# First attention of a four-layer chain: five of eight key tiles summed, all on GpSimd, and the denominators made behind the next unit's first key tile

## What is computed

```python
tokens = x.reshape(B, C, N).transpose(0, 2, 1)          # B=8, C=256, N=1024
qkv = (tokens @ w_proj + b_proj).reshape(B, N, 8, 96)   # 8 heads of 32
attn = softmax(einsum('bihd,bjhd->bijh', q, k) * 32 ** -0.5, axis=2)
res = einsum('bijh,bjhd->bihd', attn, v).reshape(B, N, 256)
out = res @ w_out + b_out + tokens
```

## Time and profile before

| | us |
|---|---|
| median of 3 executions | 3152.33 |
| the profiled execution, its own time | 3150.14 |
| its span, first to last instruction | 3148.4 |
| mean granted TensorE clock, share of full | 0.929 |
| TensorE matmul busy | 2668.8 (85%) |
| VectorE busy | 2200.9 (70%) |
| ScalarE busy | 1287.3 (41%) |
| GpSimd busy | 656.9 (21%) |

### The profile page before, as it was taken

The page is one execution under the profiler, slowest core; times in us unless marked ns, Lnnn a source line. Parts: engine busy times, 40 slices in busy tenths (PEclk is TensorE's granted clock), DMA queues, the critical chain, the costliest instruction groups (busy, mean ns, idle before and its releaser), DMA issues.

```text
span 3148.4 us, 43492 instructions
## 1 busy us (share of the span) xinstructions
PE 2668.8 (85%) x14974; PEld 1865.5 (59%) x14974; DVE 2200.9 (70%) x2403; ACT 1287.3 (41%) x1860; POOL 656.9 (21%) x405
## 2 busy tenths in 40 slices
PE   6889979899788897888879888888888898888993
PEld 4447754577545775467654676447764477644772
DVE  4776668666686676867678566785668766777666
ACT  2553325433354333543335333453334533255333
POOL 0520116102160022500225002340024300252011
PEclk8999989999899998999989999899989999999997
DMA  6100050000400004000040001300022000310016
GB/s 151 27 24 1 0 128 1 24 1 14 115 1 24 1 14 115 1 24 1 23 106 1 24 1 42 87 1 24 1 64 65 24 1 1 92 38 24 1 54 240
DMA packets 46389, 124.58 MB, mean 40 GB/s; under 512 B 9792, under 2 KB 21312, under 8 KB 42560
## 3 DMA queue, kind: packets, MB, share of 16 engines
q1 hardware_dynamic: 46144, 121.41, 14.1%
HBM read 43.01 MB, written 23.86 MB: 21 GB/s over the span
## 4 chain that ended last, share of the span: by engine, by line
PE 59%; issue 13%; DVE 11%; ACT 4%; SPq 4%; POOL 4%; DMA 3%; DVEq 0%; ACTq 0%; POOLq 0%
PE tile L1352 23%; PE pv L1352 10%; POOL acc L619 4%; PE tile L1611 4%; PE tile L1430 4%; PE tile L1456 3%; SPq L518 3%; PE pv L1466 3%; DVE small L961 3%; PE tile L1486 2%; DMA stack<-qk_r 2%; PE tile L1633 2%; PE tile L1741 2%; PE tile L1660 1%; PE tile L1511 1%
## 5 line engine op out<-in xcount | busy, mean ns | idle before, releaser
L961 DVE TENSOR_REDUCE small<-tile 128x1 f32<-128x1024 f32 x512 | 598.3, 1216 | 116.9 <-PE tile L1430 116.7
L740 ACT ACTIVATE p<-tile 128x512 f32<-128x512 f32 (+1 forms) x640 | 411.0, 684 | 247.4 <-PE tile L1456 246.0
L1430 PE MATMUL tile<-stack 96*128 96x512 f32 x1024 | 368.1, 451 | 118.4 <-DVE small L961 45.6
L1352 PE MATMUL tile<-qk_r 128*128 128x512 f32 x1536 | 377.9, 395 | 0.0
L1430 PEld LDWEIGHTS tile<-stack 96*128 96x128 f32 x1024 | 180.5, 201 | 319.7 <-DVE small L961 111.8
L619 POOL TENSOR_TENSOR acc<-acc,p 128x1024 f32<-128x1024 f32 x144 | 359.1, 2518 | 1.9
L649 POOL TENSOR_TENSOR row_sum<-act 128x256 f32<-128x256 f32 x32 | 42.1, 1335 | 1498.3 <-DVE act L1187 1498.3
L1352 PEld LDWEIGHTS tile<-qk_r 128*128 128x128 f32 x1536 | 287.1, 188 | 66.7 <-issue 7.7
L1192 DVE TENSOR_TENSOR pl<-p,ph 128x1024 fp32r<-128x1024 f32 x128 | 158.3, 1236 | 238.2 <-ACT p L834 238.2
L1466 PE MATMUL pv<-p,v 128*32 128x512 f32 x2048 | 282.7, 626 | 1.4 <-ACT p L740 1.4
L1456 PE MATMUL tile<-stack 112*128 112x512 f32 x768 | 273.3, 424 | 10.8 <-DVE rec L1009 9.2
(11 more groups left out here) (285 smaller groups left out, 4541.4 us busy)
## 6 DMA issues: line engine op xcount, KB each, us to landing
stack<-qk_r SPq DMA_DIRECT2D x192, 256.0 KB, 5.0
x_in<-in_x_dram SPq DMA_DIRECT2D x9, 1024.0 KB, 7.5
act<-in_x_dram SPq DMA_DIRECT2D x8, 1024.0 KB, 8.0
x_scratch<-act SPq DMA_DIRECT2D x7, 1024.0 KB, 4.4
z_scratch<-zbuf SPq DMA_DIRECT2D x7, 1024.0 KB, 5.2
stack<-ones SPq DMA_DIRECT2D x8, 512.0 KB, 7.6
w3f<-w3f_scratch SPq DMA_DIRECT2D x8, 512.0 KB, 3.2
fin_rest<-z_scratch SPq DMA_DIRECT2D x3, 1024.0 KB, 12.9
```

Source lines behind the costliest of these rows:

```text
L740: sc.activation(p0[:, jt % DEPTH, pair, first:first + len(heads) * HALF], tile_wait(b, "st0", *u, jt, k), ACT.Exp, scale=float(D) ** -0.5) ...
L961: ve.tensor_reduce(maxima[:, h * NT + it:h * NT + it + 1], t[:], X, ALU.max).then_inc(vector_done, vector.one("max0", g, h, it))
L1352: ins = mm(out, lhs[a][kt_], rhs[c][kt_], start=first and kt_ == 0 and m == 0, stop=last and kt_ == n - 1 and m == 2)
L1430: ins = mm(o[:, s], stack[0:IMAX, 0, g, h, it * P:(it + 1) * P], stack[0:IMAX, 1, g, h, s], start=True, stop=True)
```

## The change

It has four parts.

1. Tiles 0 to 4 are summed in units (0,0), (0,1) and (1,0), all adds on GpSimd; tiles 5, 6 and 7 go into `den0` straight from `p0`. The last unit keeps its six tiles and VectorE.
2. `den0` of these three units moves from behind `m0` to behind the score tiles of jt = 0 of the next unit, with the direct tiles first and `acc0` last. `exp0` of the tiles that overwrite p0's tiles 5 to 7 need no wait of their own then (their scores come after `den0` on TensorE).
3. In the key tiles 0 and 7 of a unit with a next one both `s0` come ahead of the four `st0`.
4. What follows `den0` moves one key tile back: `rec0` and `rows0` to jt = 1, `ex0` to jt = 2, `res`, `res_hi` and `res_lo` to jt = 3 (`res_lo` behind six adds instead of two), `out0(0)` to jt = 5, `x1` to jt = 6. `den0` of unit (1,0) now belongs to the round of all three PSUM tiles.

```diff
-SUMMED = 6
-POOL_BOTH = (1, 2, 4)
+SUMMED = 5
+SUMMED_LAST = 6
...
+def summed(g, half):
+    return SUMMED_LAST if (g, half) == UNITS[-1] else SUMMED
...
-    if jt == 0 or jt >= SUMMED:
+    if jt == 0 or jt >= summed(g, half):
         return None
-    if (g, half) == UNITS[-1]:
-        return "vector"
-    return "pool" if pair == 0 or jt in POOL_BOTH else "vector"
+    return "vector" if (g, half) == UNITS[-1] else "pool"
...
+def key_tile(g, half, jt):
+    if next_unit(g, half) and jt in (0, NT - 1):
+        return ("s0", 0), ("s0", 1), ("st0", 0), ("st0", 1), ("st0", 2), ("st0", 3)
     if next_unit(g, half):
         return ("s0", 0), ("st0", 0), ("st0", 1), ("s0", 1), ("st0", 2), ("st0", 3)
...
+            s += [("den0", *last_unit(*u))] if last_unit(*u) and jt == 0 else []
             s += [("pv0", *u, jt - 1)] if jt else []
-            s += [("ex0", *last_unit(*u))] if last_unit(*u) and jt == 1 else []
-            s += [("out0", 0)] if u == UNITS[-1] and jt == 4 else []
-        s += [("pv0", *u, NT - 1), ("m0", *next_unit(*u)), ("den0", *u)] if next_unit(*u) else (
+            s += [("ex0", *last_unit(*u))] if last_unit(*u) and jt == 2 else []
+            s += [("out0", 0)] if u == UNITS[-1] and jt == 5 else []
+        s += [("pv0", *u, NT - 1), ("m0", *next_unit(*u))] if next_unit(*u) else (
             [("den0", *u), ("pv0", *u, NT - 1)])
...
-        if kind in ("st0", "den0"):
+        if kind == "st0":
             looped = unit != UNITS[-1]
...
-        elif kind == "ex0":
+        elif kind in ("den0", "ex0"):
             looped = next_unit(*unit) not in (None, UNITS[-1])
...
-                    if jt >= SUMMED:
-                        act_e.wait_ge(tensor_done, tensor.at(b, "den0", *u))
+                    if jt >= summed(*u):
+                        assert tensor.place["den0", *u] < tensor.place["st0", *next_unit(*u), jt - DEPTH, 0]
...
+                    heads = heads_of(g, half, k)
+                    if jt == 0 and G // 2 in heads:
+                        scalar_wait("max_cols", g, half, HT - 1)
+                    o = free("st0", g, half, jt, k, but="scalar" if jt == 0 and G // 2 in heads and last_unit(g, half) else None)
...
-                    for jt in range(SUMMED - 1, NT):
+                    o, top = free("den0", g, half), summed(g, half)
+                    for jt in (*range(top, NT), top - 1):
+                        if jt >= top and (g, half) == UNITS[-1]:
+                            scalar_wait(*exp_of(g, half, jt, 1))
+                        elif jt >= top:
+                            pass
+                        elif (g, half) == UNITS[-1]:
+                            for pair in range(2):
+                                vector_wait("add0", g, half, jt, pair)
+                        else:
+                            for pair in range(2):
+                                pe.wait_ge(pool_done, gps.at(b, "add0", g, half, jt, pair))
+                        src = acc0[:, half] if jt < top else p0[:, jt % DEPTH]
```

More of the change, by code:

```diff
@@ L141, in scalar_steps @@
             s += [("exp0", *u, jt, k) for k in range(score_tiles(*u))]
-            s += [("res_hi", *last_unit(*u))] if last_unit(*u) and jt == 2 else []
+            s += [("res_hi", *last_unit(*u))] if last_unit(*u) and jt == 3 else []
     s += [("pv0_out", *UNITS[-1]), ("res_hi", *UNITS[-1])]
@@ L166, in vector_steps @@
         for jt in range(NT):
-            s += [("rec0", *last), ("rows0", *last)] if last and jt == 0 else []
-            s += [("res", *last)] if last and jt == 2 else []
-            s += [("x1", 0, ct) for ct in range(CT)] if u == UNITS[-1] and jt == 5 else []
+            s += [("rec0", *last), ("rows0", *last)] if last and jt == 1 else []
+            s += [("res", *last)] if last and jt == 3 else []
+            s += [("x1", 0, ct) for ct in range(CT)] if u == UNITS[-1] and jt == 6 else []
             for pair in range(2):
@@ L214, in pool_steps @@
     for u in UNITS:
-        for jt in range(1, SUMMED):
+        for jt in range(1, summed(*u)):
             s += [("add0", *u, jt, pair) for pair in range(2) if adder(*u, jt, pair) == "pool"]
-            s += [("res_lo", *last_unit(*u))] if last_unit(*u) and jt == 1 else []
+            s += [("res_lo", *last_unit(*u))] if last_unit(*u) and jt == 3 else []
     s += [("pool", k, ct) for k in range(10) for ct in range(CT)] + [("sm", 0)]
@@ L620, in _ @@
                                              ).then_inc(pool_done, gps.one("add0", *u, jt, pair))
-                        if jt == 1 and last_unit(*u):
+                        if jt == 3 and last_unit(*u):
                             g, half = last_unit(*u)
@@ L720, in _, with kept @@
                                   ID).then_inc(scalar_done, scalar.one("v0_kept", k))
-                def summed(u, jt, pair):
-                    if jt >= SUMMED:
-                        act_e.wait_ge(tensor_done, tensor.at(b, "den0", *u))
+                def kept(u, jt, pair):
+                    if jt >= summed(*u):
+                        assert tensor.place["den0", *u] < tensor.place["st0", *next_unit(*u), jt - DEPTH, 0]
                     elif adder(*u, max(jt, 1), pair) == "pool":
@@ L737, in exp0 @@
                         act_e.wait_ge(tensor_done, tensor.at(b, "pv0", *former[0], former[1]))
-                        summed(*former, pair)
+                        kept(*former, pair)
                     first = heads[0] % 2 * HALF
@@ L774, in _ @@
                             exp0(u, jt, k)
-                        if last and jt == 2:
+                        if last and jt == 3:
                             res_hi(*last)
@@ L1064, in _ @@
                     for jt in range(NT):
-                        if last and jt == 0:
+                        if last and jt == 1:
                             inverse0(last)
-                        elif last and jt == 2:
+                        if last and jt == 3:
                             normalise0(last)
-                        if not following and jt == 5:
+                        if not following and jt == 6:
                             x1(0)
@@ L1407, in vector_wait, with free @@
                     pe.wait_ge(vector_done, vector.at(b, *step))
-                def free(*name):
+                def free(*name, but=None):
                     for engine, count in leavers(b, *name):
+                        if engine == but:
+                            continue
                         pe.wait_ge(scalar_done if engine == "scalar" else vector_done, count)
@@ L1449, in st0 @@
                         scalar_wait("pv0_out", *last_unit(g, half))
-                    o = free("st0", g, half, jt, k)
-                    for q, h in enumerate(heads_of(g, half, k)):
+                    heads = heads_of(g, half, k)
+                    if jt == 0 and G // 2 in heads:
+                        scalar_wait("max_cols", g, half, HT - 1)
+                    o = free("st0", g, half, jt, k, but="scalar" if jt == 0 and G // 2 in heads and last_unit(g, half) else None)
+                    for q, h in enumerate(heads):
                         if jt == 0 and h < G // 2:
                             vector_wait("max_rows", g, half, h)
-                        elif jt == 0 and h == G // 2:
-                            scalar_wait("max_cols", g, half, HT - 1)
                         ins = mm(o[:, halves[q]], stack[0:K0, 1, g, h, jt * P:(jt + 1) * P],
@@ L1486, in den0 @@
                                 ins = mm(o[D * h:D * h + D, 0:P], seg, src[:, h // 2, i:i + P],
-                                         start=t == 0 and jt == SUMMED - 1, stop=t == HT - 1 and jt == NT - 1)
+                                         start=t == 0 and jt == top, stop=t == HT - 1 and jt == top - 1)
                     ins.then_inc(tensor_done, tensor.one("den0", g, half))
@@ L1537, in _ @@
                     for jt in range(NT):
-                        for kind, k in key_tile(*u):
+                        for kind, k in key_tile(*u, jt):
                             if kind == "st0":
@@ L1542, in _ @@
                                 s0(*rows_of(following, 2 * jt + k))
+                        if last and jt == 0:
+                            den0(*last)
                         if jt:
                             pv0(*u, jt - 1)
-                        if last and jt == 1:
+                        if last and jt == 2:
                             ex0(*last)
-                        if not following and jt == 4:
+                        if not following and jt == 5:
                             out0(0)
@@ L1551, in _ @@
                         m0(*following)
-                        den0(*u)
                     else:
```

11 lines of the change are left out of this document (1 added, 10 removed).

## The result

The changed kernel takes 3102.5 us (median of four runs, 3098.51 to 3105.29) against 3151.9 us; the ratio is 0.984, 95% interval 0.983 to 0.986. The forecast was 3111 us, range 3090 to 3148, faster. A second comparison on another chip gave 3101.05 us and 0.984 (0.982 to 0.986).

A forecast was written before the change was run, and what follows sets the result against it. No engine was full, TensorE nearest at 85%; above its 3.08 us tile floor lay tiles 5 and 6, slowed by VectorE's adds, and the boundary. Terms of -5.15 us per image, -41 for eight, gave 3111 us, range 3090 to 3148.

The forecast's parts named there:

- wait ahead of `m0`: TensorE's wait for tile 7's last maxima would go: -0.67 us in (0,1) and (1,0), -2.27 in (0,0).
- tile 1, tile 3: Tile 1 now holds rec0, about 3.25 us, +0.1; tile 3 takes over tile 2's wait for res, 3.47 us.
- VectorE's adds go: Tiles 5 and 6 of three units fall to 3.08 us: -1.91 and -1.61 us in (0,1).
- The boundary loses its cover: From m0 to the next unit's tile 1: two TensorE stops, 8.0 us instead of 6.29, +1.7 with den0's 0.92.
- the sum: All gains and costs over the first layer's four units: -5.15 us per image, -41 for eight images.
- Tile 7: Both s0 first: fourth score and second pv0 wait for exponentials; 4.9 us with last pv0, +0.65 each, bounds 0 and +1.
- Rival A: Clock falls at the boundary after TensorE's stops, 1.6 to 1.7 us each; 3152 us, or 3125 at one in three; chance 0.17.
- B: Slower: two low-clock stretches per boundary, m0 to tile 1; six falls cost 10.2 us per image, 3193 us; chance 0.08.
- C: GpSimd binds at the sixth add: at 3.22 us per add each unit loses 1.3 us, 3142 us; chance 0.03.
- D: Reordering costs nothing and the readers are early: three units gain 0.65 + 0.4 us more, 3086 us; chance 0.10.
- GpSimd, cost 0, cover 3.7 us: GpSimd's eight adds per unit end before exponentials and den0 need them: cost 0, 3.7 us to spare at the sixth.

The follow-up runs named there:

- e1: Kernel before with only five tiles summed and all adds on GpSimd, den0's place and the order of tiles untouched: 3083.37 us, ratio 0.976 to the kernel before.
- e3: Changed kernel without the reorder, key tiles 0 and 7 in the old order: 3065.72 us, ratio 0.971 to the kernel before; repeated at 3064.72 us, 0.973.
- e4: Changed kernel with six tiles summed instead of five, all ten adds on GpSimd: 3201.78 us, ratio 1.015 to the kernel before.
- e5: e4 with tile 5's two adds held back until VectorE's negations ahead of m0 are done, res_lo behind them: 3092.09 us, ratio 0.981 to the kernel before.
- e2: Changed kernel with six tiles summed by the engines of before, keeping den0's move, the reorder and the later steps: 3227.81 us, ratio 1.022 to the kernel before.
- e6: e5 with key tiles 0 and 7 in the old order: 3065.97 us, ratio 0.972 to the kernel before.
- e8: e6 with five tiles summed and nothing held back in unit (1,0): 3066.08 us, ratio 0.972 to the kernel before.

## Why the prediction was right

By its own steps, for unit (0,1), its own boundary at the start included:

| step | forecast | measured |
|---|---|---|
| tiles 5 and 6 | 3.08 each, full clock | 3.08, 3.08, 1.00 |
| wait ahead of `m0` | 0 | 0 |
| `den0` | 3.68 | 3.64 |
| `m0` to tile 1 | 8.0 | 8.06 |
| tile 1, tile 3 | 3.3, 3.5 | 3.28, 3.47 |
| tile 7 with last `pv0` | 4.9 | 4.58 |
| unit | 32.6 | 32.25 |

*VectorE's adds go*: right, and e1 shows that by itself it gives 3.5 us per unit less the longer `den0`. *The boundary loses its cover*: right in both stops. e1 and e3 measure the price: 8.06 us as changed, 7.18 with `den0` in its old place, 7.12 with it moved but the old order. Moving `den0` costs nothing then: the sum laid the stop to the loss of `den0` as cover, but two scores in the old order cover it as well, and only both parts together lay it bare. The reorder with `den0` in its old place was not run. *Tile 7*: right in kind, 0.3 us too long. I let the second `pv0` wait for the fourth exponential, and it did not wait. In (0,0) the sum was a gain of 2.2 and it is 2.6 without the fourth image: of the 0.7 and 0.3 for its reordered tiles 7 and 0, e3 finds 0.5 together. (1,1) lost 0.5 instead of 0.7.

Per image without falls that is 2.64 + 2.14 + 2.14 - 0.51 = 6.4 us instead of 5.15, so 51 instead of 41 for eight. *Rival A*, at 0.17, was true in part: 5 of 24 boundaries fell, at 1.67 us each, the upper end of the forecast 1.6 to 1.7, 8 us in all, and the longer low clock in one (0,0) took 2 more. So the layer gained 41 us, the figure of the sum, and 4 more lie outside it, where nothing was edited. The sum was mis-sized in one direction and the rival paid back in the other: that the two met so closely was luck. Without the falls the time would have been some 10 us less, at the lower end of the range. B did not occur as such; C did not bind; D is out, as e3 shows that the reorder costs.

One step was wrong in its reasons though not in its price: *GpSimd, cost 0, cover 3.7 us*. I took for its deadline the exponentials and `den0`, which have that much room. The nearest deadline is VectorE's first negation, which needs no result of GpSimd's: the last add ends at 521.32, it starts at 521.93. The cover is 0.6 us there and 0.5 to 0.7 over the boundaries into (0,1), (1,0) and (1,1), but for 1.5 at the end of the fourth image's (0,0). In e1 the last adds of two of the three units reach 0.4 us into this step, and it takes 0.43 to 0.45 us instead of 0.17. e4, whose two further adds overrun it, lost 99 us against the changed kernel. The 3.39 us of the earlier trace rows held that already: an add that is nearly three times its length beside GpSimd says that the two exclude each other, and every small VectorE step under a GpSimd add is then in question.

## What to carry to other kernels

When two engines lengthen each other's instructions, look for the small steps too: the deadline of the background work is the first step on the critical path that it holds up, even if no data passes between them. A wait that starts such work later can be worth much: two adds and `res_lo`, held back in e5, made 110 us. And of an edit in several parts, run each alone: here part 1 alone beats the whole, and the whole without its reorder is 37 us faster than with it.

## What the runs showed that I had not expected

- A VectorE step of 0.17 us took up to 4.15 us when it met a row of GpSimd adds, and was not let in between two of them (e4). An add of VectorE's fared the same in e2 (5.14 us, two ends passed over). What differs in the earlier trace rows, where such an add was let in at the first end, is that GpSimd's next add came 0.08 us after that end and not at once. In the first layer of e2, e4 and the kernel before this held in every such meeting, 40 without a gap and 31 with 0.08 us; in a later layer one add per image does not fit (1.64 us over an end without a gap). Why GpSimd paused was not tested.
- The granted clock fell after stops of 1.27 and 0.23 us close together in 5 boundaries and not in the others, with the same instructions. After 0.78 and 0.21 us it fell in all eight images of e6, in none of e5 at the same place, and in six of e8. A stop of 1 us can so cost 1.67 more or nothing, and edits of under 1 us per unit are hidden by it: e3, e6 and e8 are at 3065.7, 3066.0 and 3066.1 us, although two of e6's units are 0.9 us shorter than e3's. What makes the clock fall in one image and not in the next stays open.
- The time outside the first layer, untouched by any edit, is between 241.3 and 243.7 us per image on the mean, by how much low clock it holds.
